# Attention 1 of a two-layer adaLN kernel: values as the stationary operand, both heads side by side in the columns, division after a per-head out-projection

## Chip, core, metric

One NeuronCore of a Trainium2 chip runs the whole program. The metric is the device time in microseconds; the median of the runs is compared. The profiled execution is one more run of the same kernel.

## What is computed

Two transformer layers over `x` of 8 sequences x 512 tokens x 128 channels, float32. Layer 0 is a windowed attention with 16 heads and an expert layer; layer 1 is a full attention with 2 heads of 64 and a gated feed-forward with FP4-rounded operands. The change concerns layer 1's attention:

```python
q, k, v = heads(q), heads(k), heads(v)            # x: (8, 512, 128), 2 heads of 64
scores = jnp.einsum('bhqd,bhkd->bhqk', q, k) * scale
attn = jax.nn.softmax(scores, axis=-1)
out = jnp.einsum('bhqk,bhkd->bhqd', attn, v)
out = out.transpose(0, 2, 1, 3).reshape(B, T, D)
return jnp.einsum('btd,ed->bte', out, Wo)
...
x = x + ga * _L1_attn_ref(h, L1_attn_Wqkv, L1_attn_Wo)
```

Here h is the modulated layer norm of x, and ga a row of gates per sequence.

## The kernel before

The kernel runs in phases; `phase_attention1` lies between the experts and the last feed-forward. It walks over the eight sequences in eight turns written out one after another (`turns`, `body(b, par, first, next1, next2)`; `next1`: there is a next sequence, `next2`: there is one after that). A sequence has 4 tiles t of 128 queries and 2 heads j, so 8 units u = 2t + j. The order of every engine is written out by hand, with semaphores between engines.

Per unit: TensorE scores a tile for both heads at once (L1524: head j uses rows 64j to 64j+63, 512 keys as columns, one PSUM bank for each head and tile parity); VectorE takes the negated row maximum (L1678); ScalarE does the exponential with the row sum (L1588); TensorE turns the probabilities in four 128x128 transposes into one bank, psT (L1553); ScalarE copies them to `probT` (L1615); TensorE applies them to the values (L1567: `probT` is stationary, 128x128, four key chunks, 64 value columns move); VectorE multiplies the result by the reciprocal of the sum into `o` (L1721, L1726). Per tile `o` is turned (L1530) and copied (L1602) to `oT`; per sequence the out-projection (L1536) fills psQ and VectorE does the residual: times the gate, plus x, then the measurement for the next norm (L1684, L1686, L372). A float32 matmul shows as two TensorE instructions, a transpose as one.

Work on other sequences is threaded through the units: the three projections of sequence b+1 (L1509 and L1512, copied by L1598, at u = 0, 3, 5), the transposes of the norm of b+2 (L1499, L1593, at u = 7), and on VectorE the expert sum (L1668, L1669), the norm's small steps (L314 to L320) and the modulation (L354, L364, L365) of b+2 in u = 2, 3, 4, the small steps of the second norm of b-1 in u = 5 and its normalisation into h2 (L354) at the end of u = 7. GpSimd then scales and shifts h2 in two passes (L1643, L1645), and VectorE quantises it to FP4 during the next turn, ten steps, one at the end of each unit and a second one in u = 1 and u = 6; the first, the block maximum (L1071), stands in u = 0 and waits for GpSimd.

VectorE's order within a unit (left out: what is threaded in, as above; the last line is one FP4 step):

```python
nc.vector.reciprocal(rsum[:, u % 2, :], psum_[:, u % 2, :]).then_inc(rsum_ready, 1)
if u + 2 < U1 or next1:
    maxes(b, u + 2)
dve.wait_ge(applied, n + 1)
dve.wait_ge(rsum_ready, n + 1)
nc.vector.tensor_scalar(o[:, t % 2, j * D:(j + 1) * D], psO[:, j * D:(j + 1) * D], rsum[:, u % 2, :], None,
                        ALU.mult).then_inc(o_ready, 1)
...
next(steps, None)
```

## Time and profile before

| | |
|---|---|
| median of 3 runs | 1347.74 us (1344.73 to 1356.1) |
| profiled execution | 1344.88 us, its span 1343.0 us |
| granted TensorE clock, mean over the span | 0.878 of 2.4 GHz |
| TensorE busy | 995.6 us (74%) |
| VectorE busy | 808.3 us (60%) |
| ScalarE busy | 610.2 us (45%) |
| GpSimd busy | 430.8 us (32%) |

Shares are means over phases with different limits; attention 1 takes about 1016 to 1203 us of the span. "Busy" counts the time in which at least one instruction runs. In the timelines an instruction's own duration can overlap its successor's: what a step costs the engine is the distance from its start to the next start.

### The profile page before, as it was taken

The numbers are of one execution on the slowest core, as the hardware profiler recorded it, in microseconds if no ns is written. First come the engines' busy times: TensorE is split into PE (matmuls) and PEld (weight loads), VectorE is DVE, ScalarE is ACT, GpSimd is POOL, SyncE is SP. The second block draws the span as 40 slices with busy tenths as digits, with TensorE's granted clock in tenths as the row PEclk, the third lists the DMA queues.
The fourth block names the chain that finished last, engine by engine and source line by source line (L and its number), as shares of the span: only waits on it lengthen the run. The fifth ranks groups of instructions, "written<-read, shape, count | busy, mean of one in ns | idle before, by whom it ended". The sixth has DMA issues, their size and how long they took to land. (4 is left out here: it accounts for less than half of the span.)

```text
span 1343.0 us, 24963 instructions
## 1 busy us (share of the span) xinstructions
PE 995.6 (74%) x8506; PEld 674.2 (50%) x8506; DVE 808.3 (60%) x1805; ACT 610.2 (45%) x2039; POOL 430.8 (32%) x316
## 2 busy tenths in 40 slices
PE   2588989898988989898622278676608988976855
PEld 2145656565655656565521145444505666654644
DVE  4357675757586766655655814112224698868996
ACT  1157575766677676766100223132104655644422
POOL 1323242323333333321100268878530112110221
PEclk9579999998999999998655679877857999988878
DMA  8334343433434343432310214434530000000000
GB/s 256 88 76 116 98 110 101 107 96 89 120 81 113 98 109 96 111 92 57 94 35 10 57 44 73 73 62 77 98 78 1 1 1 1 1 1 0 25 14 25
DMA packets 85376, 93.61 MB, mean 70 GB/s; under 512 B 18752, under 2 KB 58032, under 8 KB 85312
## 3 DMA queue, kind: packets, MB, share of 16 engines
q1 hardware_dynamic: 73184, 81.50, 23.2%
q0 software_dynamic: 11840, 10.76, 5.1%
q8 instruction: 37, 0.61, 0.2%
q10 hardware_dynamic: 288, 0.53, 0.1%
q14 instruction: 27, 0.22, 0.1%
HBM read 24.36 MB, written 10.70 MB: 26 GB/s over the span
## 5 line engine op out<-in xcount | busy, mean ns | idle before, releaser
L743 POOL TENSOR_TENSOR qk_cos<-qk_raw,const 128x512 f32<-128x512 f32 x128 | 180.4, 1410 | 366.0 <-ACT qk_raw L567 366.0
L556 ACT ACTIVATE prob<-psS,neg_max 128x96 f32<-128x96 f32 x512 | 167.5, 342 | 66.5 <-DVE neg_max L628 66.4
L466 PE MATMUL psQ<-a_xnT,weights 128*128 128x512 f32 x256 | 153.2, 682 | 22.3 <-ACT v_tok L572 18.9
L531 PEld LDWEIGHTS psO<-probT,v_windows 96*64 96x64 f32 x2048 | 71.7, 140 | 117.5 <-ACT probT L605 92.9
L1364 POOL DMA_INDIRECT sums<-ex_y,ex_index x64 | 103.3, 1614 | 35.8 <-issue 18.6
L643 DVE TENSOR_TENSOR qk_roped<-qk_cos,qk_swapped 128x512 f32<-128x512 f32 x128 | 106.8, 834 | 5.1 <-DVE qk_swapped L634 4.6
L567 ACT COPY qk_raw<-psQ 128x512 f32<-128x512 f32 x128 | 75.5, 590 | 70.8 <-PE psQ L466 70.8
L1354 POOL DMA_INDIRECT ex_rows<-rows,ex_index x64 | 66.5, 1039 | 126.7 <-DMA ex_index<-lists 107.5
L556 ACT ACTIVATION_READ_ACCUMULATOR prob<-psS,neg_max 128x1 f32 x512 | 106.1, 207 | 0.0
L531 PE MATMUL psO<-probT,v_windows 96*64 96x64 f32 x2048 | 89.6, 231 | 21.0 <-ACT probT L605 20.4
L605 ACT COPY probT<-psT 96x512 f32<-96x512 f32 x128 | 74.8, 585 | 55.3 <-PE psT L511 55.2
L634 DVE TENSOR_TENSOR qk_swapped<-qk_swapped,const 128x512 f32<-128x512 f32 x128 | 89.9, 703 | 15.2 <-DMA qk_swapped<-qk_raw 15.1
L1300 ACT ACTIVATE ex_hidden<-ex_psH,ex_b 128x512 f32<-128x512 f32 x64 | 43.4, 687 | 118.2 <-DVE ex_index L1428 52.1
L1260 PE MATMUL ex_psH<-ex_hT,ex_w 128*128 128x512 f32 x128 | 73.7, 720 | 26.5 <-ACT ex_hidden L1300 25.0
L1567 PEld LDWEIGHTS a_psO<-a_v,a_probT 128*128 128x128 f32 x512 | 62.7, 191 | 49.7 <-ACT a_probT L1615 37.9
L661 DVE RECIPROCAL prob_rsum<-prob_sum 128x4 f32<-128x4 f32 x128 | 22.5, 176 | 107.3 <-ACT prob L556 106.2
L628 DVE TENSOR_REDUCE neg_max<-psS 128x4 f32<-128x384 f32 x128 | 70.6, 551 | 25.1 <-PE psS L453 25.1
L471 PE MATMUL psQ<-weights,a_xnT 128*128 128x256 f32 x256 | 76.9, 425 | 8.3 <-ACT qk_raw L567 2.7
L511 PE MATMUL psT<-const,prob 128*96 128x128 f32 x512 | 81.4, 283 | 1.9 <-DVE prob L662 1.9
L1567 PE MATMUL a_psO<-a_v,a_probT 128*128 128x64 f32 x512 | 69.1, 278 | 18.3 <-ACT a_probT L1615 9.5
L662 DVE TENSOR_TENSOR prob<-prob,prob_rsum 128x384 f32<-128x384 f32 x128 | 75.5, 590 | 4.4
L453 PE MATMUL psS<-qk_roped 64*64 64x96 f32 (+1 forms) x2048 | 73.8, 257 | 0.0
(300 smaller groups left out, 1935.6 us busy)
## 6 DMA issues: line engine op xcount, KB each, us to landing
qk_swapped<-qk_raw SPq DMA_DIRECT2D x512, 64.0 KB, 2.0
v_windows<-v_tok SPq DMA_DIRECT2D x32, 384.0 KB, 4.4
v_windows<-v_tok SPq DMA_DIRECT2D x32, 256.0 KB, 3.6
mod<-mod_rows SPq DMA_DIRECT2D x8, 512.0 KB, 7.4
ex_w<-in_L_ffn_W SPq DMA_DIRECT2D x16, 256.0 KB, 3.0
v_windows<-v_tok SPq DMA_DIRECT2D x32, 96.0 KB, 2.1
x<-in_L_attn_x POOLq DMA_DIRECT2D x4, 512.0 KB, 12.5
rows<-rt_h SPq DMA_DIRECT2D x8, 256.0 KB, 2.4
```

The source lines that it names most:

```text
L466: last = nc.tensor.matmul(psQ[:, :], k.wqkvT[:, col:col + P], xnT[:, :], start=True, stop=True)
L471: last = nc.tensor.matmul(psQ[:, i * 4 * D:(i + 1) * 4 * D], xnT[:, t * P:(t + 1) * P], k.wqkvT[:, col:col + 4 * D], start=(i == 0), stop= ...
L511: ins = nc.tensor.transpose(psT[0:KW, i, :], prob[:, u % 2, i, :], k.ident)
L531: ins = nc.tensor.matmul(psO[D * j:D * j + D, u % 2, i * P + a * HALF:i * P + (a + 1) * HALF], vw[:, par, a, t, hd], probT[:, 2 * j + i, a ...
L556: last = nc.scalar.activation(prob[:, s, 2 * j + i, :], psS[:, s, j, i * KW:(i + 1) * KW], ACT.Exp, bias=nmax[:, s, 2 * j + i:2 * j + i + ...
L567: ins = nc.scalar.copy(raw[:, half, :], psQ[:, :])
L634: return own.mark(nc.vector.tensor_tensor(swp[:, half, :], swp[:, half, :], k.const[:, K_SIN:K_SIN + T], ALU.mult))
L643: nc.vector.tensor_tensor(qk[:, q % 2, half // 2, half % 2, :], rcos[:, half, :], swp[:, half, :], ALU.add).then_inc(roped, 1)
L662: nc.vector.tensor_tensor(prob[:, u % 2, :, :], prob[:, u % 2, :, :], rsum[:, u % 2, :].unsqueeze(2).to_broadcast([P, 4, KW]), ALU.mult).t ...
L743: nc.gpsimd.tensor_tensor(rcos[:, half, :], raw[:, half, :], k.const[:, K_COS:K_COS + T], ALU.mult).then_inc(cos_done, 1)
L1364: nc.gpsimd.indirect_dma_start(k.sums, bass.IndirectOffsetOnAxis(ap=index2[:, par, n:n + 1], axis=0), y[:, par, n, :], None, compute_op=AL ...
L1567: last = nc.tensor.matmul(psO[:, hd], probT[:, u % 2, c, :], v[:, par, c, hd], start=(c == 0), stop=(c == TILES - 1))
```

## The change

The values become the stationary operand: the weights are a 128x64 chunk of v, the 128 queries of `probT` move, and the two heads write psO partitions 0 to 63 and 64 to 127, so that the result comes out turned and goes straight to `oT`. Nothing is divided there. Instead the out-projection is made for each head apart, into two banks (psQ and psY); VectorE scales each head's result by the reciprocal of its sums, adds the two, and only then multiplies by the gate. Both heads of a tile are applied together. `o`, its transposes and the reciprocal and division of each unit are gone; psOT's bank becomes psY.

The diff's three bodies are those of TensorE, ScalarE and VectorE, in this order. The order of work moves as well: scores run two tiles ahead, not one; the two maxima of a tile stand together in odd units; the projections of b+1 stand at tiles 0, 1, 2; the residual of b-1 is cut in three (u = 4, 5, 6) and the small steps of the second norm stand in u = 6. The third projection of b+1 waits for the residual's two reads of b-1.

```diff
             def project(b, m):
-                if m == 1:
-                    wait(pe, y_read, b - 1)
+                if m == 2:
+                    wait(pe, y_read, 2 * (b - 1))
...
-            def turn_o(b, par, t):
-                pe.wait_ge(o_ready, b * U1 + 2 * t + 2)
-                wait(pe, oT_ready, b * TILES + t)
-                nc.tensor.transpose(psOT[:, 0:P], o[:, t % 2, :], k.ident).then_inc(o_turned, 1)
+            def apply(b, par, t):
+                n = b * TILES + t
+                pe.wait_ge(probT_ready, H1 * (n + 1))
+                wait(pe, oT_ready, n)
+                if t == 0:
+                    pe.wait_ge(piece_out, 3 * b + 3)
+                for c in range(TILES):
+                    for j in range(H1):
+                        hd = slice(j * D, (j + 1) * D)
+                        last = nc.tensor.matmul(psO[hd, 0:P], v[:, par, c, hd], probT[:, j, c, :],
+                                                start=(c == 0), stop=(c == TILES - 1), skip_group_check=True)
+                last.then_inc(applied, 1)
 
             def out_project(b, par):
                 pe.wait_ge(oT_ready, (b + 1) * TILES)
-                wait(pe, piece_out, min(3 * b + 4, 3 * B))
+                wait(pe, piece_out, min(3 * b + 8, 3 * B))
+                wait(pe, y_read, 2 * b)
                 for t in range(TILES):
-                    last = nc.tensor.matmul(psQ[:, t * C:(t + 1) * C], oT[:, par, t * P:(t + 1) * P], k.w1oT[:, :],
-                                            start=(t == 0), stop=True, skip_group_check=True)
+                    for j, bank in enumerate((psQ, psY)):
+                        rows = slice(D * j, D * j + D)
+                        last = nc.tensor.matmul(bank[:, t * C:(t + 1) * C], oT[rows, par, t * P:(t + 1) * P], k.w1oT[rows, :],
+                                                start=(t == 0), stop=True, skip_group_check=True)
...
             def body(b, par, first, next1, next2):
+                for t in range(TILES):
+                    turn_prob(b, t, 0)
+                    if t + 2 < TILES or next1:
+                        pe.wait_ge(exp_done, (b * TILES + t + 1) * H1)
+                        score(b, par, t + 2)
+                    turn_prob(b, t, 1)
+                    if t < 3 and next1:
+                        project(b + 1, t)
+                    if t == 3 and next2:
+                        turn_x(b + 2)
+                    apply(b, par, t)
+                    if t == 1 and not first:
+                        out_project(b - 1, 1 - par)
...
             def body(b, par, first, next1, next2):
+                for t in range(TILES):
+                    ahead = t + 1 < TILES or next1
+                    copy_probT(b, t, 0)
+                    if ahead:
+                        exps(b, t + 1, 0)
+                    copy_probT(b, t, 1)
+                    if t < 3 and next1:
+                        piece(b + 1, 1 - par, t)
+                    if t == 3 and next2:
+                        copy_hT(b + 2)
+                    if ahead:
+                        exps(b, t + 1, 1)
+                    copy_oT(b, par, t)
...
             def residual(b):
+                dve.wait_ge(own.sem, own.mark(nc.vector.reciprocal(rsum[:, :, :], psum_[:, b % 2, :, :])))
                 dve.wait_ge(y_ready, b + 1)
-                nc.vector.tensor_tensor(ymul[:, :, :], psQ[:, :].rearrange("p (t c) -> p t c", t=TILES), ga, ALU.mult).then_inc(y_read, 1)
+                nc.vector.tensor_tensor(ymul[:, :, :], tiles(psQ), wide(rsum[:, 0, :]), ALU.mult).then_inc(y_read, 1)
+                nc.vector.tensor_tensor(yhead[:, :, :], tiles(psY), wide(rsum[:, 1, :]), ALU.mult).then_inc(y_read, 1)
+                dve.wait_ge(y_read, 2 * b + 2)
+                dve.wait_ge(own.sem, own.mark(nc.vector.tensor_tensor(ymul[:, :, :], ymul[:, :, :], yhead[:, :, :], ALU.add)))
+                yield
+                dve.wait_ge(own.sem, own.mark(nc.vector.tensor_tensor(ymul[:, :, :], ymul[:, :, :], ga, ALU.mult)))
                 dve.wait_ge(own.sem, own.mark(nc.vector.tensor_tensor(k.x[:, b, :, :], k.x[:, b, :, :], ymul[:, :, :], ALU.add)))
+                yield
                 measure(nc, k, own, b)
...
                 for u in range(U1):
                     t, j = divmod(u, H1)
-                    nc.vector.reciprocal(rsum[:, u % 2, :], psum_[:, u % 2, :]).then_inc(rsum_ready, 1)
-                    if u + 2 < U1 or next1:
-                        maxes(b, u + 2)
-                    dve.wait_ge(applied, n + 1)
-                    dve.wait_ge(rsum_ready, n + 1)
-                    nc.vector.tensor_scalar(o[:, t % 2, j * D:(j + 1) * D], psO[:, j * D:(j + 1) * D], rsum[:, u % 2, :], None,
-                                            ALU.mult).then_inc(o_ready, 1)
-                    if u == 1 and not first:
-                        residual(b - 1)
+                    if j == 1 and (t + 2 < TILES or next1):
+                        maxes(b, t + 2, 0)
+                        maxes(b, t + 2, 1)
+                    if u in (4, 5, 6):
+                        next(added, None)
```

## Rows read from the trace of the kernel before

**Rows 1.** Windows, a full turn: length, busy us of PE, PEld, DVE, ACT, POOL, clock.

```profile
1117.00:1140.00 23.00, 20.31 (x141) 14.94 (x140) 20.44 (x70) 13.39 (x32) 5.05 (x4) 1.00 0.00 1
```

**Rows 2.** Timeline (start, duration us): scores opening turns 0, 1, 2, 6; the last measurement.

```profile
1020.74 2.08 PE L1524 MATMUL a_psS<-a_kT,a_qT 64*128 64x512 f32 x4
1042.93 1.13 PE L1524 MATMUL a_psS<-a_kT,a_qT 64*128 64x512 f32 x4
...
1064.82 1.13 PE L1524 MATMUL a_psS<-a_kT,a_qT 64*128 64x512 f32 x4
...
1157.36 1.13 PE L1524 MATMUL a_psS<-a_kT,a_qT 64*128 64x512 f32 x4
...
1202.34 0.87 DVE L372 BATCH_NORM_STATS2 stats<-x 128x6 f32<-128x128 f32 x4
```

**Rows 3.** Timeline of VectorE at a turn's end; in brackets idle before, and its releaser.

```profile
1111.82 1.11 DVE L354 TENSOR_SCALAR a_h<-x,mean,rstd 128x128 f32<-128x128 f32 x4
...
1114.16 0.28 DVE L1726 TENSOR_SCALAR a_o<-a_psO,a_rsum 128x64 f32<-128x64 f32 x1 [0.57 <-PE a_psO L1567]
...
1115.65 0.69 DVE L1071 TENSOR_REDUCE a1x_amax<-a_h 128x32 f32<-128x512 f32 x1 [1.21 <-POOL a_h L1645]
...
1117.43 0.69 DVE L1684 TENSOR_TENSOR a_ymul<-a_psQ,mod 128x512 f32<-128x512 f32 x1 [0.25 <-PE a_psQ L1536]
...
1118.16 0.69 DVE L1686 TENSOR_TENSOR x<-x,a_ymul 128x512 f32<-128x512 f32 x1
```

**Rows 4.** Timeline of VectorE, unit 3 of a full turn.

```profile
1146.39 0.15 DVE L1721 RECIPROCAL a_rsum<-a_sum 128x1 f32<-128x1 f32 x1
1146.46 0.67 DVE L1678 TENSOR_REDUCE a_nmax<-a_psS 128x1 f32<-128x512 f32 x1
1147.05 0.27 DVE L1726 TENSOR_SCALAR a_o<-a_psO,a_rsum 128x64 f32<-128x64 f32 x1
1147.24 0.16 DVE L314 TENSOR_TENSOR mean<-stats 128x4 f32<-128x4 f32 x1
...
1148.01 0.68 DVE L1083 TENSOR_TENSOR a1x_xn<-a_h,a1x_inv 128x512 f32<-128x512 f32 x1
```

**Rows 5.** Timeline of TensorE and ScalarE, a tile of attention 1 (first two: turn 1).

```profile
1043.98 1.12 PE L1509 MATMUL a_psQ<-a_hT,w1qkvT 128*128 128x512 f32 x2
1045.15 0.58 ACT L1598 COPY a_qT<-a_psQ 128x512 f32<-128x512 f32 x1 [0.85 <-PE a_psQ L1509]
...
1119.88 0.60 PE L1553 MATMUL a_psT<-const,a_prob 128*128 128x128 f32 x4
1120.32 1.02 PE L1509 MATMUL a_psQ<-a_hT,w1qkvT 128*128 128x512 f32 x2
1120.52 0.58 ACT L1615 COPY a_probT<-a_psT 128x512 f32<-128x512 f32 x1 [0.17 <-PE a_psT L1553]
1121.00 0.69 ACT L1588 ACTIVATE a_prob<-a_psS,a_nmax 128x512 f32<-128x512 f32 x1
1121.17 1.08 PE L1567 MATMUL a_psO<-a_v,a_probT 128*128 128x64 f32 x8
1121.58 0.20 ACT L1588 ACTIVATION_READ_ACCUMULATOR a_prob<-a_psS,a_nmax 128x1 f32 x1
1121.67 0.59 ACT L1598 COPY a_kT<-a_psQ 128x512 f32<-128x512 f32 x1
1122.09 0.61 PE L1553 MATMUL a_psT<-const,a_prob 128*128 128x128 f32 x4
1122.63 1.13 PE L1524 MATMUL a_psS<-a_kT,a_qT 64*128 64x512 f32 x4
```

**Rows 6.** Timeline of TensorE: one application in attention 0, heads in column halves.

```profile
400.43 0.69 PE L531 MATMUL psO<-probT,v_windows 96*64 96x64 f32 x16
```

**Rows 7.** Windows of one microsecond near the stage's end, columns as in rows 1.

```profile
1194.00:1195.00 1.00, 0.52 (x5) 0.28 (x3) 0.69 (x3) 0.45 (x1) 0.00 (x0) 1.00 0.00 0
...
1202.00:1203.00 1.00, 0.00 (x0) 0.00 (x0) 0.97 (x5) 0.00 (x0) 0.00 (x0) 0.50 0.00 0
```

More of the change, by code:

```diff
@@ L1600, in copy_oT @@
             def copy_oT(b, par, t):
-                act.wait_ge(o_turned, b * TILES + t + 1)
-                nc.scalar.copy(oT[:, par, t * P:(t + 1) * P], psOT[:, 0:P]).then_inc(oT_ready, 1)
+                act.wait_ge(applied, b * TILES + t + 1)
+                wait(act, y_ready, b - 1)
+                nc.scalar.copy(oT[:, par, t * P:(t + 1) * P], psO[:, 0:P]).then_inc(oT_ready, 1)
             copy_hT(0)
@@ L1607, in _ @@
             copy_hT(1)
-            exps(0, 0)
+            exps(0, 0, 0)
+            exps(0, 0, 1)
             def body(b, par, first, next1, next2):
-                for u in range(U1):
-                    t, j = divmod(u, H1)
-                    n = b * U1 + u
-                    act.wait_ge(turned, n + 1)
-                    nc.scalar.copy(probT[:, u % 2, :, :].rearrange("p c q -> p (c q)"), psT[:, :]).then_inc(probT_ready, 1)
-                    if u + 1 < U1 or next1:
-                        exps(b, u + 1)
-                    if next1 and u in PIECE_AT:
-                        piece(b + 1, 1 - par, PIECE_AT[u])
-                    if next2 and u == 7:
-                        copy_hT(b + 2)
-                    if u == 0 and not first:
-                        copy_oT(b - 1, 1 - par, TILES - 1)
-                    if u % 2 == 0 and u > 0:
-                        copy_oT(b, par, t - 1)
-                if not next1:
-                    copy_oT(b, par, TILES - 1)
+                for t in range(TILES):
[7 more added lines that the diff above has]
+                    if t == 3 and next2:
+                        copy_hT(b + 2)
+                    if ahead:
+                        exps(b, t + 1, 1)
+                    copy_oT(b, par, t)
             turns(body)
@@ L1710, in _ @@
             modulate(1)
-            maxes(0, 0)
-            maxes(0, 1)
+            for t in range(2):
+                for j in range(H1):
+                    maxes(0, t, j)
             def body(b, par, first, next1, next2):
                 steps = quantise2(b - 2) if 0 <= b - 2 < EARLY else iter(())
+                added = iter(()) if first else residual(b - 1)
                 for u in range(U1):
                     t, j = divmod(u, H1)
-                    n = b * U1 + u
-                    dve.wait_ge(exp_done, n + 1)
-                    wait(dve, o_ready, n - 1 if u else n)
-                    nc.vector.reciprocal(rsum[:, u % 2, :], psum_[:, u % 2, :]).then_inc(rsum_ready, 1)
-                    if u + 2 < U1 or next1:
-                        maxes(b, u + 2)
-                    dve.wait_ge(applied, n + 1)
-                    dve.wait_ge(rsum_ready, n + 1)
-                    nc.vector.tensor_scalar(o[:, t % 2, j * D:(j + 1) * D], psO[:, j * D:(j + 1) * D], rsum[:, u % 2, :], None,
-                                            ALU.mult).then_inc(o_ready, 1)
-                    if u == 1 and not first:
-                        residual(b - 1)
+                    if j == 1 and (t + 2 < TILES or next1):
[3 more added lines that the diff above has]
+                        next(added, None)
                     if u == 2 and next2:
@@ L1737, in body @@
                         modulate(b + 2)
-                    if u == 5 and 0 <= b - 1 < EARLY:
+                    if u == 6 and 0 <= b - 1 < EARLY:
                         finish2(b - 1)
@@ L1745, in body @@
                 if not next1:
-                    residual(b)
+                    for _ in residual(b):
+                        pass
             turns(body)
```

81 lines of the change are left out of this document (36 added, 45 removed).

## The prediction

> **What bounds the kernel now.** The edit touches one stage, attention 1, about 1016 to 1203 us of the span, so I read that stretch alone. First the windows of one turn (one sequence): in 23 us TensorE is busy 20.3, VectorE 20.4, ScalarE 13.4 [rows 1]. Two engines stand near their limit, so freeing one cannot give much more than the other allows. Second the timeline at the turn starts: eight turns, of which the four full ones (2 to 5) go from 1064.82 to 1157.36, 23.13 us each; turn 0 takes 22.2, turn 1 21.9, turns 6 and 7 the 45.8 us to the last measurement at 1203.2 [rows 2]. Third the vector engine's waits in a full turn: 0.57 for TensorE before a division, 1.21 for GpSimd before the FP4 maximum, 0.25 for the out-projection: 2.03 in all, so 21.1 of its 23.13 us are work and handover [rows 3]. Fourth, also in the timeline, the steps of VectorE's unit [rows 4] and of TensorE and ScalarE, start to start [rows 5].
>
> **What the change takes from TensorE.** One unit's application is 8 instructions and costs 0.92 to its successor; before and after it moves few columns, yet a pass with 64 moving columns costs 0.92/8 = 0.115 us [rows 5]. After, a tile is 16 instructions with 64-column weights and 128 moving columns, the two heads in different column halves. The nearest row is attention 0's application: 16 instructions into two column halves, 64 moving columns, end within 0.69 us, at most 0.043 each [rows 6]. Bounds for the new 16: 0.7 (that row) and 16 x 0.115 = 1.84 (no overlap). Twice the moving columns of [rows 6] puts me at 0.94 a tile in place of 1.84. Gone are also four transposes of o, about 0.12 each (a transpose group of four goes 0.44 to 0.54) [rows 5]. The out-projection doubles to 16 instructions, each on one half of the rows. The scores run in such halves: 4 instructions of 512 columns take 1.05, the same as 2 of the full-height projection take by their 1.12 [rows 2, 5]. So I take 1.0 for it as before; upper bound 1.84. TensorE's own work falls by 4 x 0.9 + 0.5 = 4.1 us a turn.
>
> The Trainium skill (TensorE: Matmul & The Clock Gate, Part 3: Packing small matmuls) speaks against this: weight loads overlap running matmuls only when the row groups differ, and these two heads share all rows. By that rule the tile would stay near 1.84. The application of attention 0 has the same shared rows and still goes at 0.043 an instruction [rows 6]; so I keep 0.94 and make the rule's outcome the first rival.
>
> **The new chain of TensorE and ScalarE**, from the rows' start-to-start steps [rows 5]: transposes to their copy 0.64, copy to next ScalarE work 0.48, exponential 0.67 to ScalarE's next work (its read of the sum ends at 0.78, with a handover of 0.05 TensorE may start at 0.83), transposes to score 0.54, score 1.05 [rows 2], transposes to projection 0.44, projection to application 0.87, projection to its evacuation 1.17. The next tile's score waits for the second exponential, which stands behind the piece's copy: 1.05 + 0.44 + 1.17 + 0.48 + 0.83 = 3.97 a tile. TensorE's own order gives 0.54 + 1.05 + 0.44 + 0.87 + 0.94 = 3.84. A turn with its out-projection: 2 x 3.97 + 4.85 + 3.84 = 16.6. ScalarE's instructions stay the same in number (13.4 busy), so it isn't the bound.
>
> **What it does to VectorE.** Per unit it drops a reciprocal (0.07 to the next start) and the division (0.19) [rows 4]: 8 x 0.26 = 2.1 us a turn. It adds a reciprocal of 128x8 (one of 128x1 takes 0.15 [rows 4]; I take 0.25 with its self-wait, bounds 0.15 and 0.4), two scalings out of PSUM and an addition, with the gate's multiplication now a pass of its own. That is three 128x512 passes more; two dependent ones start 0.73 apart [rows 3], independent ones 0.6 [rows 4]: 0.25 + 0.6 + 0.73 + 0.73 = 2.3. Net +0.2 less the small waits it sheds: the work stays at 21.1.
>
> Now the stall that moves. In u=7 the vector engine normalises h2; GpSimd scales and shifts it in two passes; the FP4 maximum of the next turn's u=0 waits for them. Normalisation ends at 1111.82 + 1.11 = 1112.93, the maximum starts at 1115.65, 2.72 later, and only 1.21 of that is idle, since u=0's reciprocal, maximum and division stand between [rows 3]. After the change u=0 holds nothing but that FP4 step: the maxima have moved to odd u, reciprocal and division are gone. So 2.7 us are idle in full. A full turn of VectorE: 21.1 + 2.7 = 23.8. That is over TensorE's 16.6, and 0.7 more than today's 23.13. Behind the waiting FP4 step stand the maxima of u=1; for them wait the exponential of tile 2, behind it the second probT copy, and TensorE's application.
>
> I looked for waits of VectorE on others within such a turn. From the first maximum of u=1 (D): exponential 0.7, copy at 1.4, application 2.0, out-projection 2.9, result 4.1; the residual asks for it at D + 6.6. The scores it needs in u=5 and u=7 are there by D + 5.7 and D + 12.5, asked for at 12.2 and 18.1. So VectorE sets the pace of turns 2 to 5.
>
> **Sum, as a walk through the stage.** (1) Turn 0: at half clock a score takes 2.08, not 1.13 [rows 2]; one score more is issued up front; first transposes at 1020.1, the first tile 2.6 longer than 3.84, next tile at 1026.5; then 2 x 3.97 + 3.84: turn 1 starts at 1038.3, its tile 1 at 1042.3. (2) Turn 1: out-projection done 5.1 after that; VectorE then does scalings and sum 2.05, modulation 2.5 (1.1 and two passes of 0.7), maxima 1.25, gate and add 1.45, measure and small norm 1.6 (0.77 for the small ones [rows 4]), maxima 1.25, normalise 1.15, wait 2.7, FP4 0.6: 14.55, so D of turn 2 = 1042.3 + 19.65 = 1062.0. (3) Turns 2 to 5: 4 x 23.8 = 95.2, D of turn 6 = 1157.2. (4) Turn 6 has no expert sum (2.24: two passes and a measure of 0.8), no small norm (0.77), no modulation (2.5): 18.3 + 0.2 of waiting; D of turn 7 = 1175.7. (5) Turn 7: the last application 10.0 after D, copy, out-projection, result at 12.7, the longer residual 4.4: end 17.1 after D, 1192.8. Before it was 1203.2 [rows 2]: a gain of 10.4, call it 10. Some 13 us are gained in turns 0, 1, 6 and 7 together, the longer last residual (2.1) already taken off; turns 2 to 5 give 3 back.
>
> The profiled execution ran 1344.88 (span 1343.0 and 1.9 around it); the median of the runs is 1347.74. Minus 10: 1334.9 and 1337.7. I put 1336.
>
> The Trainium skill (TensorEngine Tiling (Array Packing), Key Properties) says that changing the tiling mode drains the array. The rows agree with a small price: transposes to score 0.54, to projection 0.44 [rows 5]. By 0.1 a change, two a tile more, the four turns not bound by VectorE would lose about 1 us together.
>
> **Rivals.**
> - *R1: the column halves do not run together.* A tile's application costs 1.84, the out-projection 1.84. For it: no row shows 128 moving columns and 128 rows in this form. Against: [rows 6]. Turns 2 to 5 hold (20 < 23.8); turn 0 loses 3.6, turn 1 2.5, turn 6 1, turn 7 4: 11 us, so the gain is gone: 1347.
> - *R2: the clock falls (the other side).* While VectorE waits and the maxima are late, TensorE stands about 2 us at a time, twice or more a turn. Against: with TensorE busy 0.52 of a microsecond the clock stayed at 1.00; for: with TensorE idle from 1202 to 1203 it stood at 0.50 (1.2 GHz) [rows 7]. At half clock its 16.6 grows to some 29 us a turn (its 14 of work twice), over 23.8: 4 x 5 to 6 more, 1358. It decides once the clock is halved for over about half of turns 2 to 5.
> - *R3: VectorE's turn is shorter than I add up*, 21 to 22 us, since the 2.03 of listed waits aren't all (each division also waits through semaphores that no row shows). Then 4 x 2 to 2.5 more is gained: 1327. Against: maximum, division and successor follow at 0.59 and 0.19 without gap in [rows 4].
> - *R4: the GpSimd wait stays 1.2 as before.* Turns 2 to 5 would take 22.3: 1330. Against: program order; nothing is left between.
>
> **How the numbers follow.** Forecast 0.56, R1 0.14, R2 0.07, R3 0.15, R4 0.08. What a measurement here can tell from no change is about 1%, 13.5 us. Forecast's own spread is about 6 us around a gain of 10 (turns 0, 1, 6, 7 by a microsecond or two each, VectorE's turn by 0.5), a quarter of it beyond 1%. Faster by over 1%: 0.56 x 0.25 + R3 + half of R4 = 0.33. Slower by over 1%: most of R2 and the tail of R1, 0.09. Within: 0.58. The range takes in R1 and R3 and leaves R2 out: 1325 to 1350.
>
> **What would show it.** Right: VectorE over 85% busy in turns 2 to 5, which last 23.5 to 24; its idle before the FP4 maximum 2.7 in place of 1.2, six times; TensorE busy under 17 of 23.8; the 16 instructions of a tile in about 1 us; turn 0 near 18. Wrong: application of 1.9 us a tile (R1), granted clock under 0.9 in 1065 to 1157 (R2), turns 2 to 5 under 22.5 (R3, R4).

## The result, and the profile after

The kernel after the change takes 1341.0 us (median of 16 runs, 1336.4 to 1345.0), the kernel before, run beside it, 1349.4 us (16 runs, 1340.1 to 1358.9): a ratio of 0.9929, 95% interval 0.9907 to 0.9950, which on 1349.4 is 9.6 us less (6.7 to 12.5); the two medians themselves are 8.4 apart. The forecast was 1336, a gain of 10.

| | before | after |
|---|---|---|
| profiled execution | 1344.88 us | 1341.86 us (span 1340.0) |
| attention 1, first score to last measurement | 187.2 us | 178.0 us |
| turns 2 to 5, one | 23.13 us | 23.82 us |
| granted TensorE clock, mean | 0.878 | 0.872 |
| TensorE, VectorE, ScalarE busy | 995.6, 808.3, 610.2 us | 979.0, 805.9, 607.8 us |

The stage is the place to read: it is 9.2 us shorter, inside the interval of the whole kernel's gain. The two profiled spans differ by 3.0 only, since the feed-forward behind the stage took 146.1 us in this execution and 139.8 in the one of before. The instructions there are the same. In the profiled executions of all the runs below that part takes 143.5 to 146.2 (e4, a variant of the kernel before, 145.0), so the 139.8 is the odd one; why it was short isn't known.

First the timeline of VectorE after: the FP4 maximum that opens turns 2, 3, 4, 6 and 7, and the last measurement (start, duration, instruction; in brackets the idle time before it and who ended it). The rows of before that answer are in [rows 3].

```profile
1059.92 0.69 DVE L1071 TENSOR_REDUCE a1x_amax<-a_h 128x32 f32<-128x512 f32 x1 [2.74 <-POOL a_h L1655]
...
1083.74 0.69 DVE L1071 TENSOR_REDUCE a1x_amax<-a_h 128x32 f32<-128x512 f32 x1 [2.73 <-POOL a_h L1655]
...
1107.56 0.69 DVE L1071 TENSOR_REDUCE a1x_amax<-a_h 128x32 f32<-128x512 f32 x1 [2.73 <-POOL a_h L1655]
...
1155.20 0.69 DVE L1071 TENSOR_REDUCE a1x_amax<-a_h 128x32 f32<-128x512 f32 x1 [2.72 <-POOL a_h L1655]
...
1174.14 0.69 DVE L1071 TENSOR_REDUCE a1x_amax<-a_h 128x32 f32<-128x512 f32 x1 [2.73 <-POOL a_h L1655]
...
1193.00 0.87 DVE L372 BATCH_NORM_STATS2 stats<-x 128x6 f32<-128x128 f32 x4
```

The starts lie 23.82 apart from turn 2 to turn 6, and each time the wait for GpSimd is 2.7; in the turns of [rows 3] it was 1.21. Next the windows of after: a full turn, turn 6 and turn 7 (length, busy us of PE, PEld, DVE, ACT, POOL, clock; compare [rows 1]).

```profile
1083.74:1107.56 23.82, 17.63 (x146) 10.90 (x144) 20.54 (x58) 13.08 (x32) 5.32 (x4) 1.00 0.00 1
...
1155.20:1174.14 18.94, 15.54 (x138) 9.87 (x136) 15.42 (x39) 12.14 (x30) 3.94 (x3) 1.00 0.00 1
1174.14:1193.87 19.73, 9.62 (x99) 7.32 (x97) 15.63 (x34) 6.43 (x16) 0.00 (x0) 0.85 0.00 0
```

VectorE is busy 20.54 of 23.82 (86%), and 2.73 of the rest is the one wait: the turn is VectorE's. TensorE fell from 20.3 to 17.6 and has 6 us to spare. Last the timeline of TensorE in turn 0, where it sets the pace; compare [rows 5] and [rows 6].

```profile
1023.17 1.09 PE L1545 MATMUL a_psO<-a_probT,a_v 128*64 128x128 f32 x16
1024.20 0.66 PE L1532 MATMUL a_psT<-const,a_prob 128*128 128x128 f32 x4
1024.79 1.13 PE L1523 MATMUL a_psS<-a_kT,a_qT 64*128 64x512 f32 x4
...
1028.91 1.13 PE L1523 MATMUL a_psS<-a_kT,a_qT 64*128 64x512 f32 x4
```

A tile's 16 instructions take 1.03 to the next start, 0.064 each; transposes to score take 0.59, and a tile 4.12 (score to score). TensorE doesn't stand idle in this tile: it is TensorE's own order, not the path through ScalarE, that sets the pace here.

### The profile page after: what moved, and what is told of

The parts are those of the page before. It is cut to its first block and busy times, and to the rows that moved or that the text cites. A ratio compares the mean times of both kernels' runs of the same rounds, so it can differ in the third digit from the quotient of the medians.

```text
span 1340.0 us, 24909 instructions
## 1 busy us (share of the span) xinstructions
PE 979.0 (73%) x8538; PEld 649.2 (48%) x8538; DVE 805.9 (60%) x1709; ACT 607.8 (45%) x2039; POOL 430.3 (32%) x316
## 3 DMA queue, kind: packets, MB, share of 16 engines
q1 hardware_dynamic: 73184, 81.50, 23.3%
## 5 line engine op out<-in xcount | busy, mean ns | idle before, releaser
L466 PE MATMUL psQ<-a_xnT,weights 128*128 128x512 f32 x256 | 152.5, 679 | 21.2 <-ACT v_tok L572 17.8
L661 DVE RECIPROCAL prob_rsum<-prob_sum 128x4 f32<-128x4 f32 x128 | 22.5, 176 | 106.1 <-ACT prob L556 105.5
L628 DVE TENSOR_REDUCE neg_max<-psS 128x4 f32<-128x384 f32 x128 | 70.5, 551 | 21.8 <-PE psS L453 21.8
L1269 PE MATMUL ex_psY<-ex_w,ex_hidden 128*128 128x128 f32 x512 | 62.1, 283 | 4.4 <-issue 4.4
```

The costliest lines, as they stand in the source:

```text
L466: last = nc.tensor.matmul(psQ[:, :], k.wqkvT[:, col:col + P], xnT[:, :], start=True, stop=True)
```

## The experiments

The stage's time below is always first score to end of the last measurement in the profiled execution, and a turn is the distance between two FP4 maxima (L1071), the first from turn 2 to turn 3. Where these stand in u = 3 (e2, e4 to e7, e9, e10), the distances from turn 5 on leave out the expert sum. Median minus stage is 1159 to 1163 us in all the kernels with more than one run, so the stage carries the differences.

### e1: one head after the other

```diff
-                for c in range(TILES):
-                    for j in range(H1):
+                for j in range(H1):
+                    for c in range(TILES):
```

> The changed kernel, but head 0's four chunks are applied before head 1's, so that the two column halves no longer alternate; nothing is left out. T (VectorE sets the pace of turns 2 to 5): a tile's application goes from 1.03 us to about 1.7 to 1.8; turns 2 to 5 stay at 23.8 (23.82 now); turns 0 and 1 get some 3 us longer each, turn 6 one, turn 7 three, so the stage's end moves from 1193.9 to about 1202 to 1204, where the kernel before has it. Rival (TensorE still sets the pace everywhere): turns 2 to 5 grow by 3 us each and the end moves by over 20 us. If the halves never overlapped, nothing moves at all.

Measured: 1343.8 us (one run); stage 181.0; turns 2 to 5 take 23.82, as in the kernel after the change. TensorE's timeline in turn 0:

```profile
1022.36 1.58 PE L1545 MATMUL a_psO<-a_probT,a_v 128*64 128x128 f32 x16
1024.46 1.13 PE L1523 MATMUL a_psS<-a_kT,a_qT 64*128 64x512 f32 x4
...
1029.07 1.13 PE L1523 MATMUL a_psS<-a_kT,a_qT 64*128 64x512 f32 x4
```

Start to next start (1023.87) is 1.51, 0.094 an instruction: alternating the column halves saves 0.5 a tile, and the tiles are 4.61 apart instead of 4.12. The sign was right, the size not: 1.51 instead of 1.7 to 1.8. The upper bound 1.84 of the forecast came from 64 moving columns with 128-column weights and was too high, so the stage lost 3.0 us in this order, not the 8 to 10 expected here or the 11 of R1. That turns 2 to 5 do not move at all shows that TensorE doesn't set them.

### e2: the FP4 steps later

The ten steps stand in u = 3 to 7, none in u = 0 to 2, so that nothing waits for GpSimd:

```diff
-                    next(steps, None)
-                    if u in (1, 6):
+                    for _ in range({3: 3, 4: 2, 5: 1, 6: 2, 7: 2}.get(u, 0)):
```

> The changed kernel, but the ten FP4 steps of a turn stand at u = 3 (three), 4 (two), 5, 6 (two), 7 (two) instead of from u = 0 on; nothing is left out. T: the 2.73 us that VectorE waits for GpSimd before the FP4 maximum are covered by the four maxima and the expert sum; turns 2 to 5 go from 23.82 to 21.1, turns 6 and 7 lose 2.5 each, the stage is 15 to 16 us shorter, the kernel about 1325 (ratio to before 0.982). Rival A (TensorE and ScalarE take over as the bound): turns stay above 22.5, under 6 us gained. Rival B (the clock falls less because TensorE is idle less): turn 7 gains 2 more than its wait.

Measured: 1326.5 us (5 runs, 1324.9 to 1327.4), ratio to the kernel before 0.9838 (0.9811 to 0.9864); stage 166.2, which is 11.8 less than after. The turns take 22.45, not 21.1 (turns 2 to 5, by their first maxima): 5.5 of the 11.8 come from these four, 3.8 from the time before turn 2's first maxima and 2.5 from turns 6 and 7 together, for which 5 had been expected. The wait had stood at six turn starts and is gone, yet 1.4 of its 2.7 came back in another form. VectorE and GpSimd at that place:

```profile
1100.78 1.28 DVE L1691 TENSOR_REDUCE a_nmax<-a_psS 128x1 f32<-128x512 f32 x2
1100.94 1.27 POOL L1653 TENSOR_TENSOR a_h<-a_h,mod 128x512 f32<-128x512 f32 x1 [3.49 <-DVE a_h L354]
1101.98 0.78 DVE L1678 TENSOR_TENSOR a_mul<-weights,mod 128x512 f32<-128x512 f32 x1
1102.30 1.60 POOL L1655 TENSOR_TENSOR a_h<-a_h,mod 128x512 f32<-128x512 f32 x1
1102.80 1.64 DVE L1679 TENSOR_TENSOR x<-x,a_mul 128x512 f32<-128x512 f32 x1
```

L1679, the same addition that takes 0.69 in after, takes 1.64 and ends half a microsecond behind GpSimd's second pass (1103.90), which itself takes 1.60 instead of 1.27. GpSimd's first pass beside the maxima out of PSUM takes its 1.27. Both kernels have the same instructions; only their order and who runs beside whom is new. Start to next start, L1679 costs 0.95 more than in after and L1678 0.16 more, 1.1 of the 1.4; the rest is order (see e7). e8 measures the dispute by itself.

Rival B was wrong: the clock fell more, not less. Once in each of turns 3, 4 and 5 TensorE stands idle for 2.25 us before the third projection:

```profile
1087.60 2.04 PE L1511 MATMUL a_psQ<-w1qkvT,a_hT 128*128 128x128 f32 x8 [2.25 <-DVE a_yhead L1702]
...
1111.09 1.97 PE L1545 MATMUL a_psO<-a_probT,a_v 128*64 128x128 f32 x16
```

The work behind it goes at half the clock in turns 3 and 4 (2.04 for 1.13, 1.97 for 1.09), not in turn 5. From maxima to maxima the turns take 22.5 all the same: where VectorE has no score or result to wait for, half a clock on TensorE costs nothing.

### e3: a third GpSimd pass

```diff
+                nc.gpsimd.tensor_tensor(spare[:, :, :], h2[:, :, :], wide(SB), ALU.add).then_inc(spared, 1)
+                pool.wait_ge(spared, b + 1)
```

> The changed kernel with one more GpSimd pass over h2 into a spare buffer between scaling and shifting (it changes nothing in the result). T: the pass of 1.3 us and its handover lie in full on the path, six times: turns 2 to 5 go from 23.82 to 25.15, the wait before the FP4 maximum from 2.73 to 4.1, the stage grows by 8. Rival (the wait costs nothing, something else sets the pace): turns stay at 23.8 and the wait grows at the cost of another idle time.

Measured: 1351.5 us (one run); stage 188.0.

```profile
1111.14 0.69 DVE L1071 TENSOR_REDUCE a1x_amax<-a_h 128x32 f32<-128x512 f32 x1 [4.08 <-POOL a_h L1658]
...
1136.31 0.69 DVE L1071 TENSOR_REDUCE a1x_amax<-a_h 128x32 f32<-128x512 f32 x1 [4.07 <-POOL a_h L1658]
```

Turns of 25.17: the pass's 1.35 goes one for one into the wait and into the turn. In these turns there is no slack behind GpSimd. The stage grew by 10.0, not 8: turn 6 is 3.4 longer, since besides the pass VectorE waits 2.25 for the out-projection there, after TensorE stood idle for 3.40 and its clock fell (0.45 in after).

### e4: the kernel before, with e2's edit

> The kernel before with the same later FP4 steps as the other kernel (3 at u = 3, then 2, 1, 2, 2). T: VectorE and TensorE hold each other there; its wait of 1.21 before the FP4 maximum goes, and turns 2 to 5 fall from 23.13 by 0.5 to 1.2, to about 22.2. Rival (TensorE alone sets the pace before): they stay at 23.1.

Measured: 1352.8 us (one run); stage 190.2; turns of 24.67, 23.42 and 23.43. Nothing was gained: the stage is 3.0 longer, the turns 0.3 to 0.7 longer than the 24.0, 23.13 and 23.13 of before, where 22.2 was expected. The single time lies within the runs of the kernel before beside it (1342.5 to 1353.2). The two lists of waits over four turns, the kernel before first (who waited <- for whom: us in all, times, longest):

```profile
DVE a_o L1726 <- PE a_psO L1567: 4.6, 6, 1.3
DVE a1x_amax L1071 <- POOL a_h L1645: 4.0, 4, 1.2
...
DVE a_ymul L1684 <- PE a_psQ L1536: 1.4, 4, 0.7
```

```profile
DVE a_o L1726 <- PE a_psO L1567: 9.2, 7, 1.4
...
DVE a_ymul L1684 <- PE a_psQ L1536: 2.6, 4, 0.7
```

The 4.0 us for GpSimd are gone and 5.8 us for TensorE have come: with u = 0 to 2 emptied, VectorE arrives at the division of u = 1 before TensorE has the product (1.39 at 1115.89). The same edit that gives 12 us after the change gives nothing before it. My reading is that the division in every unit ties VectorE to TensorE, so that time saved on the one is waited away on the other; it rests on these lists alone and wasn't tried further.

### e5: maxima beside GpSimd's passes

e2, with the normalisation of h2 ahead of the maxima of u = 7:

```diff
-                    if j == 1 and (t + 2 < TILES or next1):
+                    if j == 1 and u < 7 and (t + 2 < TILES or next1):
...
                     if u == 7 and 0 <= b - 1 < EARLY:
                         normalise2(b - 1)
+                    if u == 7 and next1:
+                        maxes(b, t + 2, 0)
+                        maxes(b, t + 2, 1)
```

> The kernel of e2_fp4_later with one move: in u=7 the normalisation into h2 stands ahead of the two maxima (per bank one pair, four passes out of PSUM, about 2.56 us together) instead of behind them, so that GpSimd's two passes (2.7 us) run beside reads of PSUM, and the two additions of the expert sum, which in e2 ran beside GpSimd (L1679 1.64 us where the changed kernel has 0.69, L1678 0.79 for 0.63), run with GpSimd idle. Theory (VectorE passes over SBUF and GpSimd's passes hold each other up): L1679 back at 0.69 to 0.73 and GpSimd's second pass (L1655) back at about 1.3; turns 2 to 5 fall from 22.45 to 21.1 to 21.4 us; the stage is 5 us shorter than e2's 166.2, the kernel about 1321. Rival 1 (the 22.45 is something else, as a coupling to TensorE or the fall of the granted clock seen once in e2): L1679 may change, but the turns stay 22.3 to 22.5 and the time is that of e2, 1326. Rival 2 (reads of PSUM by VectorE are held up by GpSimd too): the four maxima at u=7 take 1.0 or more instead of 0.68 to 0.69 and the turns stay near 22.4.

Measured: 1340.5 us (8 runs, 1337.6 to 1344.7), ratio 0.9945 (0.9927 to 0.9964); stage 180.2; turns of 23.3 to 24.0. Fourteen microseconds worse than e2. The timeline of all engines:

```profile
1105.62 2.48 DVE L1691 TENSOR_REDUCE a_nmax<-a_psS 128x1 f32<-128x512 f32 x4
...
1107.64 1.09 PE L1545 MATMUL a_psO<-a_probT,a_v 128*64 128x128 f32 x16 [4.01 <-ACT a_probT L1601]
1108.67 1.11 PE L1532 MATMUL a_psT<-const,a_prob 128*128 128x128 f32 x4
1108.98 0.69 DVE L1679 TENSOR_TENSOR x<-x,a_mul 128x512 f32<-128x512 f32 x1
1109.71 2.08 PE L1523 MATMUL a_psS<-a_kT,a_qT 64*128 64x512 f32 x4
1111.82 1.29 DVE L1691 TENSOR_REDUCE a_nmax<-a_psS 128x1 f32<-128x512 f32 x2 [1.24 <-PE a_psS L1523]
```

Of the theory the first half held: four maxima in 2.48 are not slowed, L1679 is back at 0.69, GpSimd's second pass at 1.27, and VectorE is busy 21.2 in a turn. L1678, which now meets the end of that pass, takes 0.93 instead of 0.63. The turn of 21.1 to 21.4 did not come. Rival 1 had named the fall of the clock, if not this size of it: the maxima of u = 7 stand late, TensorE runs dry for 4.01, its transposes then take 1.11 instead of 0.66 and its scores 2.08 instead of 1.13 (granted clock 0.50 from 1110 to 1111), and VectorE waits 1.24 for those scores. e9 tests it.

### e6: the second head's scaling on ScalarE

e5, with the second head's scaling as four activations on ScalarE and one combined instruction a tile on VectorE instead of three passes:

```diff
+                    last = nc.scalar.activation(yhead[:, t, :], psY[:, t * C:(t + 1) * C], ACT.Copy, scale=rsum[:, 1, t:t + 1])
...
+                    last = nc.vector.scalar_tensor_tensor(out=ymul[:, t, :], in0=psQ[:, t * C:(t + 1) * C], scalar=rsum[:, 0, t:t + 1],
+                                                          in1=yhead[:, t, :], op0=ALU.mult, op1=ALU.add)
```

> The kernel of e5_maxima_over_gpsimd with the second head's scaling by its reciprocal sums on ScalarE (four activations with a scale of one column each, at tile 2) and, on VectorE, one scalar_tensor_tensor per tile (four of 128x128) in place of two scalings and an addition of 128x512; the reciprocal stands at u=2. If VectorE sets the pace alone, its work falls from 2.05 us (0.61 + 0.71 + 0.73) to four small passes of an estimated 0.25 each, so about 1 us a turn: turns 2 to 5 from 21.2 to about 20.2, the stage 5 us shorter than e5's, the kernel about 1316. Rival: the residual now waits for ScalarE, whose order behind the second exponential delays it: VectorE idles 0.5 us or more before the first scalar_tensor_tensor, the turns stay at 21 or more and the time is e5's within 2 us.

Measured: 1351.3 us (12 runs, 1345.0 to 1356.0), ratio 1.0026 (1.0001 to 1.0051); stage 189.0; turns of 24.7 to 25.7.

```profile
1115.18 1.15 ACT L1622 ACTIVATE a_yhead<-a_psY,a_rsum 128x128 f32<-128x128 f32 x4
...
1116.47 1.13 DVE L1716 SCALAR_TENSOR_TENSOR a_ymul<-a_psQ,a_rsum,a_yhead 128x128 f32<-128x128 f32 x4 [2.90 <-ACT a_yhead L1622]
```

The rival is right in kind and far off in size: it gave the time of e5 within 2 us, and the kernel is 10.8 slower. VectorE saves 0.9 of work and waits 2.90 for ScalarE. Here the work taken off the limiting engine was worth nothing, since its result had to come back through another engine's queue. Why the loss is larger than this wait wasn't taken apart.

### e7: VectorE's order made even

e5's instructions in another order, of which the diff shows the core:

```diff
+                    if t == 1:
+                        next(added, None)
+                    if t == 3 and 0 <= b - 1 < EARLY:
+                        normalise2(b - 1)
+                    if t + 2 < TILES or next1:
+                        maxes(b, t + 2, 0)
+                        maxes(b, t + 2, 1)
...
+                        fp4(6)
```

> The kernel after the change with VectorE's order in a turn written anew, the same instructions. In e5_maxima_over_gpsimd the pairs of maxima stood so unevenly (two pairs at once, then 9 and 8 us) that TensorE ran dry for 4.0 us, its granted clock fell to half, the next scores took 2.08 instead of 1.13, and VectorE waited 1.4 and 0.5 for them. Here normalisation of h2 stands right before two pairs of maxima (u=7 and u=1) as in e5, so that GpSimd's two passes run beside reads of PSUM; then expert sum, small norm steps and six FP4 steps; scalings and sum of the residual; third pair; modulation and gate; fourth pair; measurement, second norm's small steps, the other four FP4 steps. By the rows of e5 the third pair stands some 10 us after the first, the fourth some 5 later, and the next normalisation 6 after that: TensorE's idle in one piece stays under 2 to 2.5 us. Theory (the two costs of e2 and e5 are GpSimd beside additions, and TensorE run dry): turns 2 to 5 take 21.2 to 21.8 us (e2: 22.45, e5: 23.4), L1679 stays at 0.69 and the granted clock at 1.00, the stage is 162 to 163 us (e2 166.2), the kernel 1321 to 1323. Rival: the even order makes VectorE wait elsewhere (the scalings now stand one tile earlier and ask for the out-projection some 8 us after the first pair, when TensorE may not have it): turns of 22.4 or more, no better than e2.

Measured: 1341.2 us (6 runs, 1336.8 to 1342.7), ratio 0.9931 (0.9914 to 0.9949); stage 181.1. The turns take 22.20, 22.20, 23.62, 20.63, 21.16. TensorE, the end of turns 2 and 3:

```profile
1078.86 1.09 PE L1545 MATMUL a_psO<-a_probT,a_v 128*64 128x128 f32 x16 [2.22 <-ACT a_probT L1601]
1080.47 1.13 PE L1523 MATMUL a_psS<-a_kT,a_qT 64*128 64x512 f32 x4
...
1101.06 1.30 PE L1545 MATMUL a_psO<-a_probT,a_v 128*64 128x128 f32 x16 [2.22 <-ACT a_probT L1601]
...
1103.34 2.04 PE L1523 MATMUL a_psS<-a_kT,a_qT 64*128 64x512 f32 x4
```

The same 2.22 us of idle, in the same order of work, left the clock at 1.00 the first time; the second time the application takes 1.30 instead of 1.09 and the scores behind it 2.04, and so again at the end of turns 4 and 5. The turn behind such a fall is 1.4 longer, since VectorE waits 1.4 for the out-projection. So the even order did not keep the clock.

And the theory missed at full clock too: 22.20, not 21.2 to 21.8, and only 0.25 under e2. In turn 2 VectorE waits for nobody, but it spends 1.1 more than the 21.1 of after. 0.3 is L1678, which still meets GpSimd's second pass (0.94 for 0.63). The other 0.8 is order: a step whose successor needs its result costs about 0.1 more to the next start (the FP4 maximum 0.71 here, 0.60 in after, where maxima of other data follow it), and seven steps that had one of other data behind them in after are followed by their own reader here.

The 15 us by which the stage is longer than e2's are lost for the most part in turns 6 and 7, where there is little other work: from turn 6's first maxima to the end it takes 47.6 instead of 35.5, with VectorE waiting 4.41, 2.71 and 5.54 for the out-projection, as the rival had named.

### e8: the dispute between VectorE and GpSimd by itself

The kernel after, with two spare passes behind each normalisation of h2, of three kinds in turn (an addition of two SBUF operands, a maximum over one, a multiplication of one by a constant).

> The kernel after the change with two spare VectorE passes over 512 columns right behind each of the six normalisations of h2, that is in the 2.73 us in which VectorE waits for GpSimd's two passes (1.27 to 1.3 each); results unused. Sequences 0 and 3: an addition of two SBUF operands; 1 and 4: a maximum over one SBUF operand; 2 and 5: a multiplication of one SBUF operand by a constant. Theory (a VectorE instruction with two SBUF operands and a GpSimd pass over SBUF exclude each other, with one operand they do not): the additions take 0.7 only where GpSimd hasn't begun, else up to 1.6 to 2.0, GpSimd's passes start later or take up to 1.6 to 2.0, and the FP4 maximum starts 0.6 to 1.4 later than 2.73 after the normalisation; the maxima take 0.69, GpSimd's passes 1.27 to 1.3, and the FP4 maximum still starts 2.73 behind the normalisation; the multiplications go like the maxima, unless their faster rate (0.42 a pass for FP4's steps) takes what the additions take, which is open. Rival (any VectorE access to SBUF slows GpSimd): all three kinds take longer, and the FP4 maximum comes later in all six turns.

Measured: 1346.4 us (one run). One case of each kind:

```profile
1058.60 2.37 DVE L1767 TENSOR_TENSOR a_spare<-x 128x512 f32<-128x512 f32 x2
1058.76 1.66 POOL L1654 TENSOR_TENSOR a_h<-a_h,mod 128x512 f32<-128x512 f32 x1 [1.23 <-DVE a_h L354]
1060.51 1.60 POOL L1656 TENSOR_TENSOR a_h<-a_h,mod 128x512 f32<-128x512 f32 x1
...
1083.22 1.41 DVE L1769 TENSOR_REDUCE a_spare<-x 128x4 f32<-128x512 f32 x2
1083.39 1.27 POOL L1654 TENSOR_TENSOR a_h<-a_h,mod 128x512 f32<-128x512 f32 x1 [2.77 <-DVE a_h L354]
1084.74 1.27 POOL L1656 TENSOR_TENSOR a_h<-a_h,mod 128x512 f32<-128x512 f32 x1
...
1107.11 1.83 DVE L1771 TENSOR_SCALAR a_spare<-x 128x512 f32<-128x512 f32 x2
1107.28 1.38 POOL L1654 TENSOR_TENSOR a_h<-a_h,mod 128x512 f32<-128x512 f32 x1 [2.77 <-DVE a_h L354]
1108.74 1.33 POOL L1656 TENSOR_TENSOR a_h<-a_h,mod 128x512 f32<-128x512 f32 x1
```

Two additions take 2.37 and hold GpSimd up by 0.39 and 0.33; two maxima take 1.41 and leave GpSimd's passes at 1.27; two multiplications, a pass of which goes at 0.42 among the FP4 steps, take 1.83 and cost GpSimd 0.11 and 0.06. The second round (sequences 3 to 5) repeats it within 0.01. The FP4 maximum starts 3.54, 2.82 and 2.99 behind the normalisation's end (2.73 in after). So it is not any access to SBUF: the rival falls.

The first case comes out to 0.15 us if only one of the two instructions can run at a time: the first addition runs 1058.60 to 1059.3, GpSimd's pass then its 1.27 to 1060.6 (measured 1060.42), the second addition its 0.69 from that end to 1061.1 (1060.97), and the second GpSimd pass its 1.27 from there to 1062.2 (1062.11). The Trainium skill (SBUF — State Buffer, Who interferes with whom) says just this: a VectorE instruction with two SBUF inputs and a GpSimd instruction that reads SBUF exclude each other for the whole instruction, so does a VectorE instruction in a two-port mode, which tensor_scalar can enter, and a reduction does not contend. All three cases agree with it; that the multiplication is in such a mode is read from its 0.42 alone.

### e9, e10: useless work for TensorE

e5 with three useless products of 128x512, e7 with one, where TensorE ran dry:

```diff
+                if t == 0:
+                    wait(pe, oT_ready, n)
+                    for _ in range(3):
+                        nc.tensor.matmul(psO[:, :], k.w1qkvT[:, 0:C], hT[:, :], start=True, stop=True)
```

> The kernel of e5_maxima_over_gpsimd with useless work added on TensorE: ahead of the first application of each sequence, where TensorE stood idle for 4.0 us in e5, three products of 128x512 (1.02 us each) into the bank that the application then overwrites. Nothing else differs. Theory (the late maxima of e5 cost time only because the idle TensorE lost its granted clock): the clock stays at 1.00 in turns 2 to 5, the scores after the idle piece take 1.13 instead of 2.08 and the transposes 0.66 instead of 1.12, VectorE's wait of 1.2 for these scores is gone, and the turns shorten from 23.4 to 21.7 to 22.0 us; the stage is 6 to 8 us shorter than e5's 180.2, the kernel about 1333, although TensorE does 3 us more a turn. Rival (the late maxima delay the scores by themselves, whatever the clock): VectorE's wait of 1.0 to 1.4 stays, turns 23.3 or more (TensorE has more to do), the kernel 1340 or more.

> The kernel of e7_even_order with one such useless product of 1.02 us at the same place, where TensorE stood idle for 2.2 us. In e7 the turns 2 and 3 (clock 1.00 throughout) took 22.20 us and the turns in which the clock fell after that idle piece 23.6. Theory: no fall, so all of turns 2 to 5 take 22.2 us and the stage is about 3 us shorter than e7's 181.1, and up to 3 more in turns 6 and 7; the kernel 1335 to 1338. Rival: the clock falls all the same (an idle piece of 1.2 is enough, or the rests before the other tiles), turns of 23.6 among them, the kernel 1341 as e7.

Measured, e9: 1338.2 us (6 runs, 1336.9 to 1342.8), ratio 0.9923 (0.9895 to 0.9951); stage 176.4 against 180.2 in e5; turns 22.06, 22.00, 22.00, 21.17, 19.52. The timeline at the same place as in e5:

```profile
1086.48 2.74 PE L1541 MATMUL a_psO<-a_hT,w1qkvT 128*128 128x512 f32 x6
...
1090.65 1.09 PE L1549 MATMUL a_psO<-a_probT,a_v 128*64 128x128 f32 x16 [1.44 <-ACT a_probT L1605]
...
1092.26 1.13 PE L1523 MATMUL a_psS<-a_kT,a_qT 64*128 64x512 f32 x4
...
1093.51 1.27 DVE L1695 TENSOR_REDUCE a_nmax<-a_psS 128x1 f32<-128x512 f32 x2
```

The maxima stand as late as in e5, TensorE has 2.7 us more to do, and the turn is 1.4 shorter: scores of 1.13, no wait of VectorE for them from turn 3 to turn 5. That the clock was the cost in these turns, and not the late maxima by themselves, is shown. The stage gains 3.9, not 6 to 8: the products cost 4.8 before turn 2's FP4 maximum, where TensorE sets the pace, and the later part gains 8.6.

Measured, e10: 1337.9 us (7 runs, 1334.1 to 1341.0), ratio 0.9918 (0.9889 to 0.9946); turns 22.20, 22.21, 22.20, 19.24, 19.57; stage 179.2 against 181.1. With one product of 1.02 us, leaving 1.37 idle, the scores stayed at 1.13 through turns 2 to 6; the turns that were 23.62, 20.63 and 21.16 in e7 are 1.4 to 1.6 shorter, 4.4 together. The stage gains 2.0 only, since the products cost 2.2 before turn 2's FP4 maximum, and turn 7 stayed as it was (TensorE idle for 2.22 and then at half the clock, as in e7).

### e11: the same for the kernel after the change

> The kernel after the change with one useless product of 128x512 (1.02 us on TensorE) ahead of the first application of each sequence, where TensorE stands idle for 2.04 us in turns 2 to 5 and 2.37 in turn 7; it writes a bank that the application overwrites. Theory (turn 7 took 19.1 us from its first maximum to the end instead of the 17.1 of the forecast because the clock fell to 0.50 after the 2.37 us of idle and the second application with the out-projection ran at half speed): the clock in turn 7 stays at 1.00, the out-projection's passes take 0.27 instead of 0.42, and turn 7 takes 17.3 to 18 us; turns 2 to 5, bound by VectorE and GpSimd, stay at 23.82; the stage is 1 to 2 us shorter than 178.0. Rival: the two missing microseconds are my chain's steps (the out-projection in two banks and the longer residual), not the clock: turn 7 stays at 19 and the stage at 178.

Windows of one microsecond in turn 7 of after (columns as above; the last but two is the clock); the idle stretch is 1174.4 to 1176.77:

```profile
1175.00:1176.00 1.00, 0.00 (x0) 0.00 (x0) 1.00 (x3) 0.54 (x1) 0.00 (x0) 1.00 0.00 0
...
1177.00:1178.00 1.00, 1.00 (x18) 0.81 (x16) 1.00 (x3) 0.48 (x3) 0.00 (x0) 0.86 0.00 0
1178.00:1179.00 1.00, 1.00 (x10) 1.00 (x12) 0.62 (x2) 0.18 (x1) 0.00 (x0) 0.50 0.00 0
```

Measured: 1344.7 us (one run). The clock stays at 1.00 in turn 7 while the out-projection runs, its passes take 0.27, and from its first maximum (1180.13) to the end (1197.86) the turn takes 17.7 where after has 19.1. Turns 2 to 5 stay at 23.82. The stage is not shorter (179.2), but 1.3 longer: the useless product costs 1.7 before turn 2's FP4 maximum, and turn 6 is 0.9 longer, since the clock fell there (TensorE idle for 2.05 before) and VectorE waits 1.36 for the out-projection instead of 0.45:

```profile
1165.50 0.69 DVE L1704 TENSOR_TENSOR a_ymul<-a_psQ,a_rsum 128x512 f32<-128x512 f32 x1 [1.36 <-PE a_psY L1560]
```

So the clock is 1.4 of the 2.0 us by which turn 7 missed its forecast. All of the 2.0 stands before the last application, which starts 12.0 after the first maximum where 10.0 was forecast (10.6 in e11); the other 0.6 I can't assign.

The product is no remedy in general. In turns 2, 3 and 4 of e11 the clock fell to 0.50 for some 3 us although the idle piece before was 1.72 us only (mean clock of these turns 0.93, in after 1.00), and the turns still took 23.82.

## Why the prediction was right

The gain was forecast at 10 and came at 9.6 (9.2 in the stage). The mechanism, a GpSimd wait that shows in full and makes the full turns longer while the outer turns gain, is what the runs show. The time itself came 5 us above the 1336, for the most part since the kernel before has its median at 1349.4 over 16 runs and not at the 1344.88 and 1347.74 from which I subtracted. That the sum of the gain came out so close is in part luck: turn 0 was 1.8 us too long in it and turn 7 2.0 too short, and the two cancel. Turns 2 to 5 give 2.8 back (3 forecast), the other four gain 12.0 (13).

- **Turns 2 to 5.** Forecast 23.8, measured 23.82: VectorE's work and handover unchanged at 21.1 (20.54 busy, against 20.4 of 23), plus the GpSimd wait bare at 2.7. That it is GpSimd's wait and nothing beside it, e3 shows (one more pass, 1.35 more) and e2 (without the wait the turn falls). The scalings and the sum came at 0.61, 0.71 and 0.73 and the reciprocal at 0.23, together the 2.3 of the forecast.
- **TensorE's application.** Forecast 0.94 a tile in place of 1.84, measured 1.03. The 0.94 was a choice between the bounds 0.7 and 1.84 and not worked out (twice the 0.69 of [rows 6] would be 1.38), so its closeness is luck. Out-projection 1.0, measured 1.10. A tile 3.97, measured 4.12, and not by the path that I had: I took the one through ScalarE (3.97) for the longer and TensorE's own order for 3.84, and it is TensorE's own order that takes 4.12. R1 did not come: 0.064 an instruction with the halves alternating, and even one half after the other (e1) 0.094, less than the 0.115 that I had as the bound. R1's 11 us were over three times what e1 lost. The rule of the Trainium skill (TensorE: Matmul & The Clock Gate, Part 3: Packing small matmuls) that stood behind R1 asks for different row groups; the same part also says that a load into the background weight buffer is pulled ahead. The halves here share all rows, and alternating them still saves a third; which of the two ways is at work no run shows.
- **TensorE's other steps.** Transposes to score went from 0.54 to 0.59 and to projection from 0.44 to 0.50; the forecast named 0.1 for each change of tiling mode and put no term into the sum. Projection to application takes 0.96; the sum has 0.87, where [rows 5] give 0.85. No run takes these apart.
- **Turn 0** was mis-sized: the first tile was put at 6.4 (3.84 and 2.6 for half the clock) and took 4.58 (first transposes 1019.62, next tile's 1024.20), since only its first transposes ran at half clock. Turn 1 starts at 1036.5, not 1038.3, and turn 0 lasts 16.9, not near 18. The rest of the walk to turn 2 was right (19.9 against 19.65 from turn 1's second tile).
- **Turn 7** was mis-sized the other way: 19.1, not 17.1. Here R2 happened in small: TensorE idle for 2.37, then half the clock for 3 us; 1.4 of the 2.0 (e11). I had weighed R2 for turns 2 to 5 alone, where TensorE's longest idle is 2.06 and the clock stayed at 1.00, and not for turn 7, where TensorE's work lies directly on the chain.
- **R3 and R4** fell: turns not under 23.8, the wait not 1.2.
- **"TensorE busy under 17"** was off by 0.6 (17.6), since the tile was put too short.

The walk as a whole: turn 2's first maxima at 1060.5 (forecast 1062.0), turn 6's 1155.8 (1157.2), turn 7's 1174.75 (1175.7), end 1193.9 (1192.8).

What the change leaves unused is e2: with the FP4 steps later the kernel takes 1326.5 us, 1.6% under the kernel before. No other order tried was better. The gain exists only since the change: in the kernel before, the same edit gives nothing (e4).

## What to carry to other kernels

When another engine than the edited one sets the turn, add up its work and its waits bare, as they stand once the small instructions in front of a wait are gone: here that gave the turn to 0.02 us (23.8 for 23.82). Before filling a wait with other work, look at what that work shares with the releaser (here SBUF inputs beside GpSimd), and at what it delays for the next engine: an engine with slack may lose its clock after standing idle, and then look whether anybody waits for what it does next. In e5 VectorE did, and each turn cost 1.4 more; in e2 and in turns 2 to 4 of e11 nobody did, and the turns cost nothing more.

## What the hardware did that I had not expected

- A 128x512 addition of two SBUF operands beside a GpSimd pass took 1.64 us instead of 0.69, and the GpSimd pass 1.60 instead of 1.27 (e2, e8). Maxima, over PSUM (e5) or SBUF (e8), took their usual time and left GpSimd's passes at 1.27. A multiplication by a constant at its fast rate (0.42 a pass) does cost, two of them 1.83.
- Half a clock after an idle stretch: 2.04 to 2.06 us idle left it at 1.00 (after, turns 2 to 5), 2.37 (turn 7) and 4.01 (e5) were followed by 0.50. But 2.22 and 2.25 were followed by both in one kernel (e7, e2), 3.40 left it at 1.00 once in e3 (the out-projection behind it at 0.27 a pass), and in e11 it fell after 1.72. So the length of the last idle stretch alone does not decide; what does stays open.
- 2.7 us of useless products in a turn made the turn 1.4 us shorter (e5 to e9: 23.4 to 22.0). One product a turn did the same for e7 (e10), and nothing for the kernel after the change outside turn 7 (e11).
- Sixteen passes with 64-column weights and 128 moving columns take 1.03 us when the two column halves alternate and 1.51 when they follow one another (after, e1).
